# Spectrum's input and gate from one matmul of 170 columns a band, three tiles ahead, in one pair of PSUM banks

## The chip, the cores and the metric

One core of a Trainium2 chip runs the whole program. The metric is the device time of one execution in microseconds (us), the median of several runs; less is better. The engines are TensorE (PE, with its weight loads shown apart as PEld), VectorE (DVE), ScalarE (ACT), GpSimd (POOL) and SyncE (SP, which only issues DMAs). Each runs its own queue in order and waits for others by semaphores.

## What is computed

Two layers of the same block on x of shape (4, 32, 128, 128). Cut to what matters:

```
xn = group_norm(x)                        # 32 groups: each channel of each image by itself
xm = einsum('bchw,oc->bohw', xn, W_in)    # 32 channels -> 3 * 85
x_spatial, x_freq, x_gate = split(xm, 3)
out_spatial = depthwise_conv3x3(x_spatial, W_dw)
xf  = rfft2(x_freq in patches of 8 x 8) * fft_weight
out_freq = irfft2(xf)
x = x + einsum('bchw,oc->bohw', gelu(x_gate) * (out_spatial + out_freq), W_out)
```

The projection into x_spatial is merged with the depthwise convolution into one set of weights. The Fourier transform of a patch is a matmul with a basis over its pixels, and back another.

## The kernel before

**Tiles.** The image lies in SBUF with 128 partitions = 4 bands of 32 columns (q = 0 to 3) x 32 channels. A strip is 8 columns of each band over all 128 rows; there are 4 strips an image, 16 a layer, 32 in all. A strip has 8 tiles (TPS) of 16 rows x 8 columns = 128 pixels a band; 128 tiles (LT) a layer, 256 in all. A tile's matmuls take the pixels of one band as the stationary operand (128 x 128, with the high and low fp16 parts of the normalized input stacked on the partitions) and weights as the moving one, 85 columns (HID) a band. So a result of a tile is 128 pixels x 340 columns (GC, 4 bands x 85).

**What a tile goes through.** The names are the tiles of the trace.
- `ps_u` (L346): the input of the spectrum, four matmuls of 85 columns, one a band. ACT makes `uh` of it, its high fp16 part (L500), and DVE `ul`, the low part (L790, which reads `ps_u` and `uh`).
- `ps_z` (L406, 407, 409): three matmuls of 340 columns with the basis `bas`, on `uh`, `uh` and `ul`. DVE multiplies by the spectrum's weights into `y` (L796), ACT makes `yh` (L509) and POOL `yl` (L570).
- `ps_s` (L340): 7 matmuls of 85 columns a band for the convolution (`conv(i, q)`), then three of 340 with `inv` on `yh`, `yh` and `yl` (L414, 415, 417).
- `ps_g` (L346): the gate, four matmuls of 85 columns, from which ACT makes `g`, the gelu (L504). DVE multiplies `f` = `ps_s` x `g` (L764).
- `ps_ft` (L375): four transposes of `f`, which ACT copies to `ft` (L494). `ps_o` (L383): the output projection, once for two tiles, and DVE adds it to x (L774).

**The order.** Each engine runs the same loop over steps i = -3 to 259 (`steps()`, `live(i, offset)` says whether tile i + offset exists), each with its part written in a fixed order. PE in step i: conv of band 0 of tile i; transposes of tile i-2; in even steps `ps_o` of tiles i-4 and i-3; two of the four gate matmuls of tile i; conv of band 1; `ps_u` of tile i+3; the other two gate matmuls of tile i; conv of band 2; `ps_z` of tile i+2; conv of band 3; the three inverse matmuls into `ps_s`. ACT: `ft` of tile i-2, `uh` of i+3, `g` of i, `yh` of i+2. DVE: `f` of i-1, in odd steps the residual, `ul` of i+3, `y` of i+2. POOL: `yl` of i+2.

**Work beside the tiles.** The next strips' inputs are made in a strip's steps (`staged`): DVE normalizes (`norm`, L705, and an image's outer columns in L713) in step 0 of the strip, ahead of `ul`; ACT makes the high parts (`parts` L472) at the end of steps 1, 3 and 5, and DVE the low ones (L721) in steps 2, 4 and 6 ahead of `ul`, when ACT's copy is done. SP loads these into the `stack` tiles. In layer 0 DVE also makes statistics: two `bn_stats` (L669) in step 3 of each strip ahead of `ul`, for the strip that layer 0 has finished, and at the end of some early steps those of images 2 and 3 (L658), for which in step 1 it waits until the sums of image 1 have been sent: a DMA that POOL issues in step 0 behind `yl`. Layer 1's weights are merged on DVE and ACT (`scale`, `merge`, `hi_of_projection`, `hi_of_taps` and others, one each in steps 39 to 63) and laid out by ACT in 14 pieces (`placing`, L444, L451, L456) at the end of steps 7 and 0 of seven strips (steps 64 to 120).

**Buffers.** PSUM has eight banks, all in use: `ps_s` 2, `ps_u` 2, `ps_g`, `ps_z`, `ps_ft`, `ps_o` one each. `uh`, `ul`, `y`, `yh`, `yl`, `f`, `g` have two buffers each.

Of the kernel before, what the change touches and what calls it, by code (L numbers as in the profile page):

```python
# [7 lines left out]
F32 = mybir.dt.float32  # L8
F16 = mybir.dt.float16
I32 = mybir.dt.int32  # L10
ALU = mybir.AluOpType
# [28 lines left out]
HI, LO = 0, 1  # L40
LEAD = 3
DRAIN = 4
WARM = 40
KH = P * (P // 2 + 1)

# [30 lines left out]
def build(nc, x_in, edges_in, w_raw, w_fft, w_out, basis, inverse, eye32, fold, sums, y_out):  # L76
    ctx = ExitStack()
    with ctx:
        def sb(name, shape, dt=F32):
            return ctx.enter_context(nc.sbuf_tensor(name, shape, dt))  # L80

        def sem(name):
            return ctx.enter_context(nc.semaphore(name))
# [48 lines left out]

        uh = sb("uh", [128, 2, GC], F16)
        ul = sb("ul", [128, 2, GC], F16)
        g = sb("g", [128, 2, GC])
        y32 = sb("y32", [128, 2, GC])
        yh = sb("yh", [128, 2, GC], F16)
        yl = sb("yl", [128, 2, GC], F16)
# [3 lines left out]
        def bank(name):  # L142
            return ctx.enter_context(nc.psum_tensor(name, [128, 512], F32))
        ps_s = [bank("ps_s0"), bank("ps_s1")]
        ps_u = [bank("ps_u0"), bank("ps_u1")]
        ps_g, ps_z, ps_ft, ps_o = (bank(n) for n in ("ps_g", "ps_z", "ps_ft", "ps_o"))

        s_id = sem("s_id")
        s_basis = sem("s_basis")
# [46 lines left out]
        s_y = sem("s_y")  # L196
        s_yh = sem("s_yh")
        s_yl = sem("s_yl")
        s_gate = sem("s_gate")
        s_gelu = sem("s_gelu")  # L200
        s_s = sem("s_s")
        s_f = sem("s_f")
# [110 lines left out]
        def _(pe):  # L313
            mm = nc.tensor.matmul
            pe.wait_ge(s_id, 16)
            for l in range(LAYERS):
                pe.wait_ge(s_amax, l + 1)
                nc.tensor.transpose(ps_g[0:3, 128 * l:128 * l + 128], amax[:, l, :], id32[:, :]).then_inc(s_turned, 1)
                if l == 0:
                    pe.wait_ge(s_fold_in, 16)  # L320
                mm(ps_u[l][:, 0:HID], fold_sb[:, :], fft[l][:, :], start=True, stop=True).then_inc(s_fold, 1)
                pe.wait_ge(s_spread, l + 1)
                mm(ps_z[:, 4 * l:4 * l + 3], ones[:, :], spread[:, l, :], start=True, stop=True).then_inc(s_top, 1)
            pe.wait_ge(s_basis, 32)
# [6 lines left out]
            def pixels(kind, i, q, dy, rows=128):  # L331

                at = TW * (1 + TH * (i % TPS) + dy)
                return stack[(i // TPS) % 2][0:rows, kind, q, at:at + PIX]
# [5 lines left out]
                    mm(ps_s[i % 2][:, HID * q:HID * (q + 1)], pixels(kind, i, q, dy, rows), w[0:rows, m, :],  # L340
                       start=(q == 0 and m == 0), stop=False)

            def project(bank, which, i, bands):

                for q in bands:
                    t = mm(bank[:, HID * q:HID * (q + 1)], pixels(A, i, q, 0), pw[layer(i)][:, which, :],  # L346
                           start=(q == 0), stop=(q == Q - 1))
                return t

            def stacks_loaded(strip, kind):  # L350

# [10 lines left out]
            for i in steps():  # L362
# [21 lines left out]
                               start=True, stop=True)  # L384
                    o.then_inc(s_o, 1)
                if live(i, 0):
                    need(pe, s_gelu, i)
                    project(ps_g, 1, i, range(Q // 2))
                    conv(i, 1)
                if live(i, 3):  # L390
                    if (i + 3) % TPS == 0:
                        stacks_loaded((i + 3) // TPS, 0)
                    if (i + 3) % LT == 0:
                        pe.wait_ge(s_ready, PLACED * layer(i + 3) + PROJECTIONS)
                        pe.wait_ge(s_weff, LAYERS)
                    need(pe, s_uh, i + 2)
                    need(pe, s_ul, i + 2)
                    project(ps_u[(i + 3) % 2], 0, i + 3, range(Q)).then_inc(s_u, 1)
                if live(i, 0):
                    project(ps_g, 1, i, range(Q // 2, Q)).then_inc(s_gate, 1)  # L400
                    conv(i, 2)
                if live(i, 2):
                    k = i % 2
# [16 lines left out]
        def _(act):  # L420
# [66 lines left out]
            for i in steps():  # L487
                if i < 0:
                    for part in staged(i, {1: 1, 3: 3, 5: 5})[1]:
                        hi_part(1, ORDER[part // 2])  # L490
                if live(i, -2):
                    need(act, s_ftp, i - 1)
                    need(act, s_o, (i - 6) // 2 + 1)
                    nc.scalar.activation(ft[:, (i - 2) % 4, :, :].rearrange("p q n -> p (q n)"), ps_ft[0:HID, 0:Q * 128],  # L494
                                         ACT.Copy).then_inc(s_ft, 1)
                if live(i, 3):
                    k = (i + 3) % 2
                    need(act, s_u, i + 4)
                    need(act, s_z, i + 2)
                    nc.scalar.activation(uh[:, k, :], ps_u[k][:, 0:GC], ACT.Copy, scale=US).then_inc(s_uh, 1)  # L500
                if live(i, 0):
                    need(act, s_gate, i + 1)
                    need(act, s_f, i - 1)
                    nc.scalar.activation(g[:, i % 2, :], ps_g[:, 0:GC], ACT.Gelu,  # L504
                                         scale=gsc[layer(i)][:, 0:1]).then_inc(s_gelu, 1)
                if live(i, 2):
                    need(act, s_y, i + 3)
                    need(act, s_s, i + 1)
                    nc.scalar.activation(yh[:, i % 2, :], y32[:, i % 2, :], ACT.Copy).then_inc(s_yh, 1)  # L509
                strip, mine = staged(i, {1: 1, 3: 3, 5: 5})  # L510
                if i >= 0:
                    for part in mine:
                        hi_part(strip, ORDER[part // 2])

                if i == 40:
                    hi_of_projection(1)
                if i == 48:
                    hi_of_taps(1)
                if 64 <= i < LT - 8 and i % TPS in (0, TPS - 1):
                    placing(1, 2 * (i // TPS - 8) + (i % TPS == TPS - 1))  # L520
# [66 lines left out]
        def _(dve):  # L587
# [16 lines left out]
            def turned(l):  # L604

                dve.wait_ge(s_turned, l + 1)
                link(v.tensor_reduce(top[:, l:l + 1], ps_g[0:3, 128 * l:128 * l + 128], AX.X, ALU.max))
                dve.wait_ge(s_id, 16)
                v.tensor_scalar(spread[:, l, :], id32[0:3, 0:3], top[:, l:l + 1], None, ALU.mult).then_inc(s_spread, 1)

# [32 lines left out]

            def spectrum(l):
                dve.wait_ge(s_fold, l + 1)
                v.tensor_scalar(weff[l][:, :], ps_u[l][:, 0:HID], ip2[:, l, 1:2], 1.0 / (BS * BS * US),
                                ALU.mult, ALU.mult).then_inc(s_weff, 1)

            def image_stats(b, n):
# [108 lines left out]
            for i in steps():  # L758
                if live(i, -1):
                    k = (i - 1) % 2  # L760
                    need(dve, s_s, i)
                    need(dve, s_gelu, i)
                    need(dve, s_ftp, i - 2)
                    v.tensor_tensor(f[:, k, :], ps_s[k][:, 0:GC], g[:, k, :], ALU.mult).then_inc(s_f, 1)  # L764
                if live(i, -5) and i % 2 == 1:
                    tile = i - 5
                    l, b, k = place(tile // TPS)
# [17 lines left out]
                        lo_part(strip, ORDER[part // 2 - 1])  # L785
                if live(i, 3):
                    k = (i + 3) % 2
                    need(dve, s_uh, i + 4)
                    need(dve, s_z, i + 2)
                    v.scalar_tensor_tensor(ul[:, k, :], ps_u[k][:, 0:GC], US, uh[:, k, :],  # L790
                                           ALU.mult, ALU.subtract).then_inc(s_ul, 1)
                if live(i, 2):
                    k = i % 2
# [94 lines left out]
```

## Time and profile before

| | before |
|---|---|
| median of 3 runs | 861.08 us (860.65 to 861.73) |
| the profiled execution | 862.21 us, span 860.3 us, mean granted clock 0.989 |
| PE busy | 818.8 us, 95% of the span |
| PEld | 665.4 us, 77% |
| DVE | 616.5 us, 72% |
| ACT | 579.9 us, 67% |
| POOL | 264.7 us, 31% |
| the chain of work that ended last | PE 93%, DMA 3%, DVE 1%, ACT 1% |

The span runs from the first to the last instruction of the profiled execution. The chain goes back from the last instruction, at each step to what released it; its shares say which engine the end waited for. In a timeline row the first number is the start and the second the length; matmuls and the elementwise operations of ACT and DVE are pipelined, so that the next one starts before the last has ended: what one costs on a full queue is the distance from start to start, not its length.

### The profile page before, as it was taken

What the parts mean: (1) busy time and instruction counts of PE and PEld (TensorE: products, weight loads), DVE (VectorE), ACT (ScalarE), POOL (GpSimd) and SP (SyncE); (2) the same over time, 40 slices, a digit from 0 to 9 for tenths busy, and PEclk for the clock granted to TensorE, in tenths of its full rate; (3) what the DMA queues carried; (4) which work ended last, traced back from release to release, by engine and by line L of the source; (5) the groups of instructions that cost most, each with busy time, mean ns of one, the idle gap of its engine ahead of it and who ended that gap; (6) DMA issues with size and microseconds to landing.
All of it is one profiled execution on the core that took longest, in us unless ns stands there. A gap on an engine that the chain in (4) does not pass through costs nothing.

```text
span 860.3 us, 32550 instructions
## 1 busy us (share of the span) xinstructions
PE 818.8 (95%) x12850; PEld 665.4 (77%) x12850; DVE 616.5 (72%) x1198; ACT 579.9 (67%) x1154; POOL 264.7 (31%) x335
## 2 busy tenths in 40 slices
PE   1379999999999999999999999999999999999997
PEld 0258888888788888888888888878888888888886
DVE  6657877788787876778777776777766777667543
ACT  3246677666767777776776777677777767777664
POOL 1223224343334322243223422222222222232221
PEclk9969999999999999999999999999999999999999
DMA  7695446554445655544565555556565555655521
GB/s 268 139 252 153 116 114 144 126 131 114 114 116 115 145 123 126 118 117 105 116 139 134 126 132 144 135 129 154 136 153 148 132 129 133 160 133 147 134 77 51
DMA packets 65505, 115.66 MB, mean 134 GB/s; under 512 B 15874, under 2 KB 17066, under 8 KB 64970
## 3 DMA queue, kind: packets, MB, share of 16 engines
q1 hardware_dynamic: 62470, 109.71, 51.9%
q0 software_dynamic: 1904, 2.31, 1.1%
q8 instruction: 104, 1.70, 0.9%
q10 hardware_dynamic: 980, 1.55, 0.7%
q14 instruction: 47, 0.39, 0.1%
HBM read 11.01 MB, written 8.59 MB: 23 GB/s over the span
## 4 chain that ended last, share of the span: by engine, by line
PE 93%; DMA 3%; DVE 1%; ACT 1%; issue 1%; SPq 1%; POOL 0%; ACTq 0%; DVEq 0%; POOLq 0%
PE ps_s L340 34%; PE ps_ft L375 14%; PE ps_o L383 8%; PE ps_g L346 6%; PE ps_u L346 5%; PE ps_s L414 4%; PE ps_z L406 4%; PE ps_s L417 4%; PE ps_s L415 4%; PE ps_z L409 4%; PE ps_z L407 4%; DMA sums<-st 1%; DMA stack<-parts 1%; DMA id<-in_eye 1%; SPq L249 1%
## 5 line engine op out<-in xcount | busy, mean ns | idle before, releaser
L340 PE MATMUL ps_s<-cw,stack 128*128 128x85 f16 (+1 forms) x7168 | 458.8, 203 | 3.7 <-DVE f L764 3.7
L340 PEld LDWEIGHTS ps_s<-cw,stack 128*128 128x128 f16 (+1 forms) x7168 | 381.5, 99 | 53.2 <-DVE f L764 4.1
L570 POOL TENSOR_TENSOR yl<-y,yh 128x340 f16<-128x340 f32 x256 | 224.7, 878 | 561.2 <-ACT yh L509 561.2
L509 ACT ACTIVATE yh<-y 128x340 f16<-128x340 f32 x256 | 124.7, 487 | 206.0 <-DVE y L796 121.5
L790 DVE SCALAR_TENSOR_TENSOR ul<-ps_u,uh 128x340 f16<-128x340 f32 x256 | 130.0, 508 | 116.6 <-ACT uh L500 116.6
L721 DVE TENSOR_TENSOR parts<-xn,parts 128x1024 f16<-128x1024 f32 x96 | 117.5, 1226 | 90.0 <-ACT parts L472 90.0
L375 PE MATMUL ps_ft<-id,f 128*85 128x128 f32 x1024 | 163.1, 282 | 0.2 <-ACT ft L494 0.2
L494 ACT ACTIVATE ft<-ps_ft 85x512 f32<-85x512 f32 x256 | 149.7, 585 | 17.2 <-PE ps_ft L375 14.8
L764 DVE TENSOR_TENSOR f<-ps_s,g 128x340 f32<-128x340 f32 x256 | 129.1, 504 | 15.5 <-PE ps_s L417 5.4
L504 ACT ACTIVATE g<-ps_g,gsc 128x340 f32<-128x340 f32 x256 | 137.7, 538 | 0.8 <-PE ps_g L346 0.5
L500 ACT ACTIVATE uh<-ps_u 128x340 f16<-128x340 f32 x256 | 115.2, 450 | 22.8 <-PE ps_u L346 22.7
L796 DVE TENSOR_TENSOR y<-ps_z,weff 128x340 f32<-128x340 f32 x256 | 128.3, 501 | 1.3 <-PE ps_z L409 1.3
L346 PE MATMUL ps_g<-pw,stack 128*128 128x85 f16 x1024 | 126.0, 206 | 0.0
L346 PEld LDWEIGHTS ps_g<-pw,stack 128*128 128x128 f16 x1024 | 75.2, 99 | 53.4 <-issue 51.9
L375 PEld LDWEIGHTS ps_ft<-id,f 128*85 128x85 f32 x1024 | 115.2, 155 | 0.7 <-DVE f L764 0.7
L472 ACT ACTIVATE parts<-xn 128x1024 f16<-128x1024 f32 x96 | 99.9, 1043 | 15.1 <-issue 10.4
L346 PE MATMUL ps_u<-pw,stack 128*128 128x85 f16 x1024 | 81.9, 202 | 4.6 <-DMA stack<-parts 4.6
L383 PE MATMUL ps_o<-ft,wo 85*32 85x256 f32 x1024 | 81.8, 391 | 0.7 <-ACT ft L494 0.7
L406 PE MATMUL ps_z<-uh,bas 128*128 128x340 f16 x256 | 79.4, 310 | 2.3 <-DVE y L796 1.9
L414 PE MATMUL ps_s<-yh,inv 128*128 128x340 f16 x256 | 79.1, 309 | 0.0
L409 PE MATMUL ps_z<-ul,bas 128*128 128x340 f16 x256 | 79.1, 309 | 0.0
L407 PE MATMUL ps_z<-uh,bas 128*128 128x340 f16 x256 | 78.9, 308 | 0.0
(77 smaller groups left out, 632.8 us busy)
## 6 DMA issues: line engine op xcount, KB each, us to landing
stack<-parts SPq DMA_DIRECT2D x502, 130.0 KB, 2.6
stack<-parts SPq DMA_DIRECT2D x128, 65.0 KB, 2.0
out_y<-yo SPq DMA_DIRECT2D x16, 512.0 KB, 2.9
stack<-parts SPq DMA_DIRECT2D x124, 64.5 KB, 2.0
stack<-parts SPq DMA_DIRECT2D x124, 64.0 KB, 2.0
x<-in_x SPq DMA_DIRECT2D x3, 2048.0 KB, 10.1
x<-in_x SPq DMA_DIRECT2D x4, 512.0 KB, 6.9
gathered<-sums POOLq DMA_DIRECT2D x32, 24.0 KB, 2.7
```

What stands on the lines that cost most here:

```text
L340: mm(ps_s[i % 2][:, HID * q:HID * (q + 1)], pixels(kind, i, q, dy, rows), w[0:rows, m, :], start=(q == 0 and m == 0), stop=False)
L346: t = mm(bank[:, HID * q:HID * (q + 1)], pixels(A, i, q, 0), pw[layer(i)][:, which, :], start=(q == 0), stop=(q == Q - 1))
L375: t = nc.tensor.transpose(ps_ft[0:HID, q * 128:(q + 1) * 128], f[:, k, HID * q:HID * (q + 1)], id32[:, :])
L383: o = mm(ps_o[C * q:C * q + C, 0:256], wo[layer(i - 4)][:, :], ft[:, k:k + 2, q, :], start=True, stop=True)
L494: nc.scalar.activation(ft[:, (i - 2) % 4, :, :].rearrange("p q n -> p (q n)"), ps_ft[0:HID, 0:Q * 128], ACT.Copy).then_inc(s_ft, 1)
L504: nc.scalar.activation(g[:, i % 2, :], ps_g[:, 0:GC], ACT.Gelu, scale=gsc[layer(i)][:, 0:1]).then_inc(s_gelu, 1)
L509: nc.scalar.activation(yh[:, i % 2, :], y32[:, i % 2, :], ACT.Copy).then_inc(s_yh, 1)
L570: nc.gpsimd.tensor_tensor(yl[:, k, :], y32[:, k, :], yh[:, k, :], ALU.subtract).then_inc(s_yl, 1)
L721: v.tensor_tensor(part[:, LO], xn[:, :, 1 + dx:1 + dx + TW], part[:, HI], ALU.subtract).then_inc(s_xl, 1)
L764: v.tensor_tensor(f[:, k, :], ps_s[k][:, 0:GC], g[:, k, :], ALU.mult).then_inc(s_f, 1)
L790: v.scalar_tensor_tensor(ul[:, k, :], ps_u[k][:, 0:GC], US, uh[:, k, :], ALU.mult, ALU.subtract).then_inc(s_ul, 1)
L796: v.tensor_tensor(y32[:, k, :].rearrange("p (q o) -> p q o", q=Q), ps_z[:, 0:GC].rearrange("p (q o) -> p q o", q=Q), weff[layer(i + 2)][:, ...
```

## The change

One matmul of 170 columns a band makes the spectrum's input and the gate together (`pw` holds both sets of weights side by side), four a tile instead of eight of 85. They write `ps_ug`, two banks of PSUM in one tensor: band q at column 256 q, its first 85 columns the spectrum's input (`ps_u`, now a view of it) and the next 85 the gate (`ps_g`). There is one such pair of banks, no second buffer, and no bank `ps_g` of its own; seven banks are used.

The projection of tile i+3 stays where `ps_u`'s was in step i, behind conv of band 1; both gate pieces of tile i go away. PE waits ahead of it for `ul` and `g` of tile i+2. On ACT `g` of tile i+3 follows `uh` of tile i+3 at once, under the same wait for `s_u`. On DVE `ul` waits for `g` of its tile instead of `uh`, so that ACT and DVE don't read the pair of banks together. `g` has five buffers (AHEAD = LEAD + 2), since `f` uses it four steps later; `f` no longer waits for `s_gelu`. Operations that read `ps_ug` go over four runs of 85 elements. Two small matmuls and a transpose at the program's start write other banks.

PE, a step without `ps_o`, before, from the start of conv of band 0:

```order
L340 MATMUL ps_s<-cw,stack 128x85 [waits s_f]
L340 MATMUL ps_s<-cw,stack 128x85 x6
L375 MATMUL ps_ft<-id,f 85x128 [waits s_ft,s_f]
L375 MATMUL ps_ft<-id,f 85x128 x3
L346 MATMUL ps_g<-pw,stack 128x85 [waits s_gelu]
L346 MATMUL ps_g<-pw,stack 128x85
L340 MATMUL ps_s<-cw,stack 128x85 x7
L346 MATMUL ps_u<-pw,stack 128x85 [waits s_ul,s_uh]
L346 MATMUL ps_u<-pw,stack 128x85 x3
L346 MATMUL ps_g<-pw,stack 128x85 x2
L340 MATMUL ps_s<-cw,stack 128x85 x7
```

and the same place now:

```order
L344 MATMUL ps_s<-cw,stack 128x85 [waits s_f]
L344 MATMUL ps_s<-cw,stack 128x85 x6
L380 MATMUL ps_ft<-id,f 85x128 [waits s_ft,s_f]
L380 MATMUL ps_ft<-id,f 85x128 x3
L344 MATMUL ps_s<-cw,stack 128x85 x7
L351 MATMUL ps_ug<-pw,stack 128x170 [waits s_gelu,s_ul]
L351 MATMUL ps_ug<-pw,stack 128x170 x3
L344 MATMUL ps_s<-cw,stack 128x85 x7
```

Eight matmuls in three places have become four in one, and its waits are for the tile before, in the same banks.

DVE, one step's `ul` and `y` and what stands ahead and behind, before:

```order
L721 TENSOR_TENSOR parts<-xn,parts 128x1024 [waits s_xh,s_xn]
L790 SCALAR_TENSOR_TENSOR ul<-ps_u,uh 128x340 [waits s_z,s_uh]
L796 TENSOR_TENSOR y<-ps_z,weff 128x340 [waits s_yl,s_z]
L764 TENSOR_TENSOR f<-ps_s,g 128x340 [waits s_ftp,s_gelu,s_s]
L774 SCALAR_TENSOR_TENSOR x<-ps_o,osc,x 128x32x8 [waits s_o]
```

and now:

```order
L722 TENSOR_TENSOR parts<-xn,parts 128x1024 [waits s_xh,s_xn]
L790 SCALAR_TENSOR_TENSOR ul<-ps_ug,uh 128x340 [waits s_z,s_gelu]
L797 TENSOR_TENSOR y<-ps_z,weff 128x340 [waits s_yl,s_z]
L764 TENSOR_TENSOR f<-ps_s,g 128x340 [waits s_ftp,s_s]
L774 SCALAR_TENSOR_TENSOR x<-ps_o,osc,x 128x32x8 [waits s_o]
```

The order is the same; the wait for `g` has moved from `f` to `ul`. ACT's order (`ft`, `uh`, `g`, `yh`, `parts`) is unchanged too.

```diff
-        ps_u = [bank("ps_u0"), bank("ps_u1")]
-        ps_g, ps_z, ps_ft, ps_o = (bank(n) for n in ("ps_g", "ps_z", "ps_ft", "ps_o"))
+        ps_z, ps_ft, ps_o = (bank(n) for n in ("ps_z", "ps_ft", "ps_o"))
+        ps_ug = ctx.enter_context(nc.psum_tensor("ps_ug", [128, 1024], F32))
+        bands = ps_ug[:, :].rearrange("p (q n) -> p q n", q=Q)
+        ps_u, ps_g = bands[:, :, 0:HID], bands[:, :, HID:2 * HID]
...
-            def project(bank, which, i, bands):
-                for q in bands:
-                    t = mm(bank[:, HID * q:HID * (q + 1)], pixels(A, i, q, 0), pw[layer(i)][:, which, :],
-                           start=(q == 0), stop=(q == Q - 1))
-                return t
+            def project(i):
+                for q in range(Q):
+                    at = 256 * q
+                    t = mm(ps_ug[:, at:at + 2 * HID], pixels(A, i, q, 0), pw[layer(i)][:, :, :],
+                           start=(q % 2 == 0), stop=(q % 2 == 1))
+                t.then_inc(s_u, 1)
...
                 if live(i, 0):
-                    need(pe, s_gelu, i)
-                    project(ps_g, 1, i, range(Q // 2))
                     conv(i, 1)
                 if live(i, 3):
...
-                    need(pe, s_uh, i + 2)
-                    need(pe, s_ul, i + 2)
-                    project(ps_u[(i + 3) % 2], 0, i + 3, range(Q)).then_inc(s_u, 1)
+                    need(pe, s_ul, i + 3)
+                    need(pe, s_gelu, i + 3)
+                    project(i + 3)
                 if live(i, 0):
-                    project(ps_g, 1, i, range(Q // 2, Q)).then_inc(s_gate, 1)
                     conv(i, 2)
...
                     need(act, s_u, i + 4)
                     need(act, s_z, i + 2)
-                    nc.scalar.activation(uh[:, k, :], ps_u[k][:, 0:GC], ACT.Copy, scale=US).then_inc(s_uh, 1)
-                if live(i, 0):
-                    need(act, s_gate, i + 1)
-                    need(act, s_f, i - 1)
-                    nc.scalar.activation(g[:, i % 2, :], ps_g[:, 0:GC], ACT.Gelu,
-                                         scale=gsc[layer(i)][:, 0:1]).then_inc(s_gelu, 1)
+                    nc.scalar.activation(uh[:, k, :].rearrange("p (q o) -> p q o", q=Q), ps_u, ACT.Copy,
+                                         scale=US).then_inc(s_uh, 1)
+                    need(act, s_f, i + 4 - AHEAD)
+                    nc.scalar.activation(g[:, (i + 3) % AHEAD, :].rearrange("p (q o) -> p q o", q=Q), ps_g,
+                                         ACT.Gelu, scale=gsc[layer(i + 3)][:, 0:1]).then_inc(s_gelu, 1)
...
                     need(dve, s_s, i)
-                    need(dve, s_gelu, i)
                     need(dve, s_ftp, i - 2)
-                    v.tensor_tensor(f[:, k, :], ps_s[k][:, 0:GC], g[:, k, :], ALU.mult).then_inc(s_f, 1)
+                    v.tensor_tensor(f[:, k, :], ps_s[k][:, 0:GC], g[:, (i - 1) % AHEAD, :], ALU.mult).then_inc(s_f, 1)
...
-                    need(dve, s_uh, i + 4)
+                    need(dve, s_gelu, i + 4)
                     need(dve, s_z, i + 2)
-                    v.scalar_tensor_tensor(ul[:, k, :], ps_u[k][:, 0:GC], US, uh[:, k, :],
+                    v.scalar_tensor_tensor(ul[:, k, :].rearrange("p (q o) -> p q o", q=Q), ps_u, US,
+                                           uh[:, k, :].rearrange("p (q o) -> p q o", q=Q),
                                            ALU.mult, ALU.subtract).then_inc(s_ul, 1)
```

## Rows read from the trace of the kernel before

**Rows 1.** The page, part 1: busy us, share of the span, instructions.
```profile
PE 818.8 (95%) x12850; PEld 665.4 (77%) x12850; DVE 616.5 (72%) x1198; ACT 579.9 (67%) x1154; POOL 264.7 (31%) x335
```

**Rows 2.** The list of waits: who for whom, total us, times, longest.
```profile
PE ps_s L340 <- DVE f L764: 3.7, 1, 3.7
```

**Rows 3.** The timeline of PE, steps 119 to 121: start, length, operation.
```profile
401.48 0.64 PE L375 MATMUL ps_ft<-id,f 128*85 128x128 f32 x4
...
402.32 0.32 PE L346 MATMUL ps_u<-pw,stack 128*128 128x85 f16 x4
402.47 0.24 PE L346 MATMUL ps_g<-pw,stack 128*128 128x85 f16 x2
402.55 0.45 PE L340 MATMUL ps_s<-cw,stack 128*128 128x85 f16 x7
402.84 0.31 PE L406 MATMUL ps_z<-uh,bas 128*128 128x340 f16 x1
...
403.27 0.45 PE L340 MATMUL ps_s<-cw,stack 128*128 128x85 f16 x7
...
404.27 0.64 PE L375 MATMUL ps_ft<-id,f 128*85 128x128 f32 x4
...
407.74 0.64 PE L375 MATMUL ps_ft<-id,f 128*85 128x128 f32 x4
```

**Rows 4.** The timeline of ACT, steps 119 to 126.
```profile
402.67 0.46 ACT L500 ACTIVATE uh<-ps_u 128x340 f16<-128x340 f32 x1
...
414.14 0.49 ACT L509 ACTIVATE yh<-y 128x340 f16<-128x340 f32 x1 [0.86 <-DVE y L796]
...
421.13 0.58 ACT L494 ACTIVATE ft<-ps_ft 85x512 f32<-85x512 f32 x1
421.61 0.44 ACT L500 ACTIVATE uh<-ps_u 128x340 f16<-128x340 f32 x1
421.95 0.54 ACT L504 ACTIVATE g<-ps_g,gsc 128x340 f32<-128x340 f32 x1
423.05 0.49 ACT L509 ACTIVATE yh<-y 128x340 f16<-128x340 f32 x1 [0.56 <-DVE y L796]
423.44 1.04 ACT L472 ACTIVATE parts<-xn 128x1024 f16<-128x1024 f32 x1
424.39 0.57 ACT L494 ACTIVATE ft<-ps_ft 85x512 f32<-85x512 f32 x1
```

**Rows 5.** The timeline of DVE, steps 122 to 126.
```profile
413.61 0.50 DVE L796 TENSOR_TENSOR y<-ps_z,weff 128x340 f32<-128x340 f32 x1
...
416.16 0.49 DVE L790 SCALAR_TENSOR_TENSOR ul<-ps_u,uh 128x340 f16<-128x340 f32 x1
...
422.08 0.51 DVE L790 SCALAR_TENSOR_TENSOR ul<-ps_u,uh 128x340 f16<-128x340 f32 x1 [0.57 <-ACT uh L500]
422.51 0.50 DVE L796 TENSOR_TENSOR y<-ps_z,weff 128x340 f32<-128x340 f32 x1
...
424.58 1.23 DVE L721 TENSOR_TENSOR parts<-xn,parts 128x1024 f16<-128x1024 f32 x1 [1.10 <-ACT parts L472]
425.73 0.50 DVE L790 SCALAR_TENSOR_TENSOR ul<-ps_u,uh 128x340 f16<-128x340 f32 x1
```

**Rows 6.** The timeline of ACT around a piece of layer 1's weights.
```profile
379.21 0.49 ACT L509 ACTIVATE yh<-y 128x340 f16<-128x340 f32 x1 [0.69 <-PE ps_s L417]
...
380.16 0.59 ACT L494 ACTIVATE ft<-ps_ft 85x512 f32<-85x512 f32 x1
```

**Rows 7.** The timeline of DVE from step 47 to 48.
```profile
203.36 0.50 DVE L796 TENSOR_TENSOR y<-ps_z,weff 128x340 f32<-128x340 f32 x1
...
206.86 0.50 DVE L790 SCALAR_TENSOR_TENSOR ul<-ps_u,uh 128x340 f16<-128x340 f32 x1
```

**Rows 8.** The timelines of DVE and PE at the first steps.
```profile
59.49 0.69 DVE L658 BATCH_NORM_STATS2 st<-x 128x6 f32<-128x512 f32 x1 [5.45 <-DMA sums<-st]
...
60.66 0.68 PE L340 MATMUL ps_s<-cw,stack 128*128 128x85 f16 x7 [3.73 <-DVE f L764]
```

More of the change, by code:

```diff
@@ L42 @@
 DRAIN = 4
+AHEAD = LEAD + 2
 WARM = 40
@@ L134, in build @@
         ul = sb("ul", [128, 2, GC], F16)
-        g = sb("g", [128, 2, GC])
+        g = sb("g", [128, AHEAD, GC])
         y32 = sb("y32", [128, 2, GC])
@@ L198, in build @@
         s_yl = sem("s_yl")
-        s_gate = sem("s_gate")
         s_gelu = sem("s_gelu")
@@ L317, in _ @@
                 pe.wait_ge(s_amax, l + 1)
-                nc.tensor.transpose(ps_g[0:3, 128 * l:128 * l + 128], amax[:, l, :], id32[:, :]).then_inc(s_turned, 1)
+                nc.tensor.transpose(ps_o[0:3, 128 * l:128 * l + 128], amax[:, l, :], id32[:, :]).then_inc(s_turned, 1)
                 if l == 0:
                     pe.wait_ge(s_fold_in, 16)
-                mm(ps_u[l][:, 0:HID], fold_sb[:, :], fft[l][:, :], start=True, stop=True).then_inc(s_fold, 1)
+                mm(ps_ug[:, HID * l:HID * l + HID], fold_sb[:, :], fft[l][:, :], start=True, stop=True).then_inc(s_fold, 1)
                 pe.wait_ge(s_spread, l + 1)
@@ L606, in turned @@
                 dve.wait_ge(s_turned, l + 1)
-                link(v.tensor_reduce(top[:, l:l + 1], ps_g[0:3, 128 * l:128 * l + 128], AX.X, ALU.max))
+                link(v.tensor_reduce(top[:, l:l + 1], ps_o[0:3, 128 * l:128 * l + 128], AX.X, ALU.max))
                 dve.wait_ge(s_id, 16)
@@ L645, in spectrum @@
                 dve.wait_ge(s_fold, l + 1)
-                v.tensor_scalar(weff[l][:, :], ps_u[l][:, 0:HID], ip2[:, l, 1:2], 1.0 / (BS * BS * US),
+                v.tensor_scalar(weff[l][:, :], ps_ug[:, HID * l:HID * l + HID], ip2[:, l, 1:2], 1.0 / (BS * BS * US),
                                 ALU.mult, ALU.mult).then_inc(s_weff, 1)
```

## The prediction

> **What bounds the kernel now.** I read the page first: TensorE (PE) is busy 95% of the span, ScalarE (ACT) and VectorE (DVE) 67% and 72% [rows 1]. Then the list of waits: once its loads are in, PE waits only for `f`, once, 3.7 us [rows 2]; all else that waits is ACT, DVE or POOL. So from about 61 us on PE sets the time. The PE timeline gives its beat: the transposes start at 401.48, 404.27 and 407.74, so a step without the `ps_o` matmuls takes 2.79 us and one with them 3.47 us, 6.26 for two tiles, 25.04 for the eight tiles of a strip and 801 for 32 strips [rows 3]. The work around it (loads, first steps, last transposes and store) makes 860.3. The median of the runs, 861.1, lies 0.8 above this span and the profiled run's own time, 862.2, 1.9 above; I add what the sum gives for the span to the median.
>
> **The change on PE.** A step had eight matmuls of 85 columns. Start to start the four into `ps_u` take 0.15 us, the two into `ps_g` behind them 0.08, the two ahead 0.09, in all 0.32, 40 ns each; seven conv matmuls take 0.29, 41 ns each. The three of 340 columns from 402.84 on take 0.43, 0.145 each [rows 3]. A 170-column one has no row. It lies between half of a 340 one (72 ns) and two 85 ones (80 ns); a straight line through both sizes gives 40 + (145 - 40) x 85/255 = 75 ns, nearly what I take, 74, because the 340 spacing alternates 0.14 and 0.15. Four are 0.296: 0.024 us a step less, between 0 and 0.033. PE's strip becomes 25.04 - 0.19 = 24.85, its two steps 2.77 and 3.44.
>
> A rule of the Trainium skill speaks here too. The rows show 85 columns at 40 to 41 ns and 340 at 145 ns [rows 3]. "TensorE: Matmul & The Clock Gate", section "Back-to-back issue gap", gives the gap of a matmul alone as columns/2.4 + 2.5 ns. An estimate by it is 38, 73 and 144 ns for 85, 170 and 340 columns, so four for eight would give back only 0.01 us a step (2.5 us in all) against 0.024 by the rows; the 85-column row contradicts it by 2 to 3 ns and the 340 row agrees. The same section gives some 81 ns for 128 columns in a stream of weight loads and matmuls, which these rows don't show.
>
> **The change elsewhere, which decides.** Three waits change. PE may write the one pair of banks for tile i+3 only when both `ul` and `g` of tile i+2 are made (before: two `ps_u` banks, a tile more of slack). `g` of tile i+3 is now made directly behind `uh` of it. And DVE's `ul` waits for `g`, no longer for `uh`. Behind `ul` on DVE stands `y`; behind `y` waits ACT's `yh`, and behind `yh` on ACT stand the `parts` copy, `ft` and the next `uh`. So there is now a ring ft, uh, g (ACT), ul, y (DVE), yh (ACT), ft, through which each tile must go, and in which ACT can't work on anything else while DVE makes `ul` and `y`. Before, `g` ran on ACT (421.95) while DVE made `ul` (422.08) [rows 4, 5]: `g` was no part of the ring.
>
> Its price, start to start, from rows where the next instruction had nothing to wait for: ft to uh 0.48, uh to g 0.34, g 0.54 long [rows 4], hand-over to DVE 0.03 (uh ends 422.05, ul starts 422.08), ul to y 0.43 [rows 5], y 0.50 long, hand-over back 0.03 (413.61 + 0.50, yh at 414.14), yh to the next on ACT 0.39 [rows 4]. Sum 2.74 us. A `parts` copy adds 0.95 three times in a strip [rows 4]. The `lo` part on DVE that follows it hides: copy 1.04 + 0.03, then 1.14 to `ul` [rows 4, 5], is 2.21, against 0.95 + 0.48 + 0.34 + 0.57 = 2.34 on ACT. So the ring takes 8 x 2.74 + 2.85 = **24.77 us a strip**, against 24.85 for PE: a tie. Without `g` in it it had been some 0.44 a step shorter (`ul` started 0.03 after `uh`'s end), 21.3 a strip.
>
> Does PE wait in a plain strip? `uh` starts 0.35 after PE's first `ps_u` matmul (402.32, 402.67 [rows 3, 4]), now 0.15 later for four of 74 ns: P + 0.50. `ul` starts at P + 1.41 and ends at P + 1.92, and PE can go on about 0.1 later (an estimate: the hand-over of 0.03 and a weight load), at P + 2.0, where its own next projection stands at P + 2.77. The slack is 0.77. From step 0 to 6 of a strip the ring takes 6 x 2.74 + 2.85 = 19.29 and PE 3 x 2.77 + 3 x 3.44 = 18.63; the lag of 0.66 just fits. So in layer 1, where ACT and DVE have only this, PE still bounds: -0.19 a strip. That ring and PE are within 0.1 us a strip is the weak place of this forecast.
>
> In layer 0 other work stands in the ring:
> - Once a strip (steps 11 to 131) DVE makes two `bn_stats` ahead of `ul`: y 413.61 to ul 416.16 is 2.55 by DVE alone [rows 5], against 0.53 + 0.39 + 0.48 + 0.34 + 0.57 = 2.31 by ACT. +0.24: strip 25.0, longer than PE's 24.85, about what it was before (-0.05).
> - In steps 64 to 120 ACT writes layer 1's weights, two pieces a strip, 14 in all. The one between 379.21 and 380.16 costs 380.16 - 379.21 - 0.39 = 0.56 [rows 6]; the fourteen read so cost 0.31 to 0.56 and come to 6.4, 0.91 a strip. Before, they lay in ACT's idle time (0.69 ahead of each `yh` [rows 6]). Strip 25.9, +0.87, for 7 strips **+6.1**.
> - Single pieces. The longest is in step 48, where statistics, the merging of the taps and a norm with its edge stand on DVE between `y` and `ul`: 206.86 - 203.36 = 3.50, over 2.31 by 1.2 [rows 7]. Read in the same way, DVE's step 40 costs 1.0, and ACT's `vh` and `wh` of layer 1 0.7 and 0.3. +3.2 in all.
>
> The sum: start of the program +0.7 (0 to 2: `yl` of tile 2 comes later by the `g` in the ring, behind it on POOL stands the DMA of the sums, whose landing DVE and then PE await until 59.49 and 60.66 [rows 8]); plain strips 16 x -0.19 = -3.0, and -0.5 for the last three tiles' gates, which are made earlier; six and a half strips with statistics -0.3; weights +6.1; single pieces +3.2; going from PE's beat to the ring's and back once gains 2.77 - 2.0 = -0.7. Together **+5.5**: span 865.8, median 866.6.
>
> **Nothing for:** the dropped wait of `f` for `g` (`g` is now three tiles early), the five `g` buffers, and the startup matmuls in other banks (before 42 us PE waits for loads anyway). The reads of `ps_ug` in four runs of 85 have no row; the `parts` copies, whose input goes in runs of 8 elements, cost 0.95 for 1024 elements, as contiguous `ft` costs 0.48 for 512 [rows 4], so I take nothing, and 10 ns an operation as an upper bound, 30 ns a step.
>
> **Rivals.**
> (1) Ends faster: PE stays the bound throughout, because ACT's pieces are absorbed. It decides if the ring is at least 0.15 us a step shorter than 2.74 (the 25.9 of the weights' strips less 24.85, by 8). For it: PE's beat is rock steady now, and an error of 20 ns a step moves 2.5 us of layer 0. Against: `yh` can't start before `y`, and the queue orders are unchanged. It gives -0.024 x 253 = -6 and the last gates -0.5: 854.6.
> (2) Near no change: the ring is 20 to 40 ns a step shorter, or half of the single pieces hide: 866.6 - 3 - 2.5 = 861 to 862.
> (3) Clearly slower: the ring costs 30 ns a step more (reads in four runs, or waits between ACT and DVE that cost more when both are always late). A strip's ring is then 25.0, 0.16 over PE's, so it bounds layer 1 too: 16 x 0.16 = 2.6 there and 16 x 0.24 = 3.8 in layer 0 on top of the forecast: 873.
> (4) The change doesn't do what it says: a 170-column matmul costs 80 ns as two of 85. Then layer 1 is as before: +3.5, 870.
>
> **How the numbers follow.** The forecast (863 to 870, with (4) inside it) has 0.48, (3) 0.12, (2) 0.18, (1) and what lies between 854 and 859 0.22. The time is 866.6; the range 855 to 875 leaves out the outer parts of (1) and (3). What a measurement can tell from no change is 0.2%, 1.7 us. Slower 0.60, same 0.17, faster 0.23.
>
> **What would show it.** Right: matmuls into `ps_ug` come every 74 ns; in layer 0 PE waits at the projection for `ul`, most between 258 and 432 us, where a strip takes 25.9; in layer 1 a strip takes 24.85 with hardly a wait; ACT's `yh` waits for `y` at every step. Wrong: no waits in layer 0 (rival 1), or waits in layer 1 too (rival 3); strips of 25.04 there with none (4).

## The result, and the profile after

| | before | changed |
|---|---|---|
| median | 861.0 us (860.65 to 861.73) | 871.6 us (870.68 to 871.91) |
| profiled execution, its span | 862.2, 860.3 us | 871.8, 870.0 us |

The changed kernel takes 1.012 of the time before (95% interval 1.0103 to 1.0138): slower by 10.6 us. The forecast was slower, by 5.5 (866.6). The spans of the two profiled executions differ by less than the medians, 9.7 us, because the one before ran 1.2 above its median and the changed one 0.2.

The page of the changed kernel, parts 1 and 4, against [rows 1]:

```profile
PE 819.4 (94%) x11826; PEld 661.1 (76%) x11826; DVE 608.8 (70%) x1198; ACT 555.9 (64%) x1154; POOL 263.4 (30%) x335
PE 67%; ACT 13%; DVE 9%; issue 7%; DMA 2%; SPq 1%; ACTq 0%; DVEq 0%; POOL 0%; POOLq 0%
```

By busy time nothing has become the bound: PE is still at 94%, ACT and DVE are even a little less busy. But the chain of work that ended last was 93% PE before and is 67% PE now, with 13% of ACT and 9% of DVE in it. The list of waits, whose counterpart is [rows 2] (who for whom, us in total, times, longest):

```profile
ACT yh L510 <- DVE y L797: 265.1, 253, 5.6
DVE ul L790 <- ACT g L505: 143.8, 131, 7.0
PE ps_ug L351 <- DVE ul L790: 6.4, 13, 1.5
```

`yh` waits for `y` in 253 of its 256 times (135 before), and `ul` now waits for `g`. PE's own waits look small, because a matmul that waits for a few tenths of a us behind a pipelined predecessor is partly counted as busy (an example is below). The start of the first projection matmul of every eighth tile shows them better. From those starts in the two traces:

| stretch (tiles) | before, us | changed, us | difference | forecast |
|---|---|---|---|---|
| to tile 8 | 70.58 | 71.47 | +0.9 | +0.7 |
| 8 to 64: statistics, single pieces | 175.26 | 178.71 | +3.5 | +2.9 |
| 64 to 128: weights of layer 1 | 200.29 | 207.88 | +7.6 | +6.1 |
| 128 to 248: layer 1 | 375.60 | 373.84 | -1.8 | -2.9 |
| rest, to the end | 38.6 | 38.1 | -0.5 | -0.5, -0.1 for the strip in it, and -0.7 for the change of bound |
| span | 860.3 | 870.0 | +9.7 | +5.5 |

The places are those of the forecast. Every one of the sizes came out on the slow side of it, by 0.2, 0.6, 1.5, 1.1 and 0.8 us (the 0.7 for the change of bound has no place of its own and stands in the last row).

The ring in the timeline of ACT, then of DVE, in layer 1 (steps 176 and 177; before: [rows 4, 5]):

```profile
617.91 0.45 ACT L502 ACTIVATE uh<-ps_ug 128x340 f16<-128x340 f32 x1
618.26 0.54 ACT L505 ACTIVATE g<-ps_ug,gsc 128x340 f32<-128x340 f32 x1
619.79 0.49 ACT L510 ACTIVATE yh<-y 128x340 f16<-128x340 f32 x1 [1.00 <-DVE y L797]
620.18 0.57 ACT L496 ACTIVATE ft<-ps_ft 85x512 f32<-85x512 f32 x1
```
```profile
618.83 0.51 DVE L790 SCALAR_TENSOR_TENSOR ul<-ps_ug,uh 128x340 f16<-128x340 f32 x1
619.26 0.50 DVE L797 TENSOR_TENSOR y<-ps_z,weff 128x340 f32<-128x340 f32 x1
```

`g` ends at 618.80, `ul` starts 0.03 later, `y` ends at 619.76 and `yh` starts 0.03 later: ACT stands idle for 1.00 us between `g` and `yh`, and so in every plain step. `uh` took 0.45 and `g` 0.54 as before, though they read four runs of 85 across two banks.

Two of PE's stretches, one in layer 1 (step 171) and one in the strips with weights (step 75):

```profile
601.51 0.46 PE L351 MATMUL ps_ug<-pw,stack 128*128 128x170 f16 x4
601.80 0.45 PE L344 MATMUL ps_s<-cw,stack 128*128 128x85 f16 x7
```
```profile
294.55 0.45 PE L344 MATMUL ps_s<-cw,stack 128*128 128x85 f16 x7
295.30 0.47 PE L351 MATMUL ps_ug<-pw,stack 128*128 128x170 f16 x4 [0.30 <-DVE ul L790]
```

Four matmuls of 170 columns take 0.29 us (601.51 to 601.80). In the second, the seven conv matmuls are through 0.29 after 294.55, and the projection starts 0.75 after it: some 0.46 us lost, of which the row shows 0.30 as idle.

### The profile page after: what moved, and what is told of

The parts are those of the page before. It is cut to its first block, busy times and chain, and to the rows that moved or that the text cites. A ratio compares the mean times of both kernels' runs of the same rounds, so it can differ in the third digit from the quotient of the medians.

```text
span 870.0 us, 30247 instructions
## 1 busy us (share of the span) xinstructions
PE 819.4 (94%) x11826; PEld 661.1 (76%) x11826; DVE 608.8 (70%) x1198; ACT 555.9 (64%) x1154; POOL 263.4 (30%) x335
## 4 chain that ended last, share of the span: by engine, by line
PE 67%; ACT 13%; DVE 9%; issue 7%; DMA 2%; SPq 1%; ACTq 0%; DVEq 0%; POOL 0%; POOLq 0%
PE ps_s L344 25%; PE ps_ft L380 10%; PE ps_ug L351 7%; PE ps_o L388 6%; DVE y L797 4%; ACT ft L496 3%; ACT parts L474 3%; PE ps_s L416 3%; PE ps_z L408 3%; ACT g L505 3%; PE ps_s L417 3%; PE ps_s L419 3%; PE ps_z L409 3%; PE ps_z L411 3%; ACT uh L502 2%
## 5 line engine op out<-in xcount | busy, mean ns | idle before, releaser
L344 PEld LDWEIGHTS ps_s<-cw,stack 128*128 128x128 f16 (+1 forms) x7168 | 392.3, 99 | 106.9 <-issue 51.9
L790 DVE SCALAR_TENSOR_TENSOR ul<-ps_ug,uh 128x340 f16<-128x340 f32 x256 | 130.5, 510 | 144.4 <-ACT g L505 143.8
L496 ACT ACTIVATE ft<-ps_ft 85x512 f32<-85x512 f32 x256 | 147.3, 575 | 4.5 <-PE ps_ft L380 4.3
L505 ACT ACTIVATE g<-ps_ug,gsc 128x340 f32<-128x340 f32 x256 | 137.0, 535 | 0.3
L351 PE MATMUL ps_ug<-pw,stack 128*128 128x170 f16 x1024 | 118.8, 238 | 15.6 <-DVE ul L790 6.4
L502 ACT ACTIVATE uh<-ps_ug 128x340 f16<-128x340 f32 x256 | 112.6, 440 | 7.7 <-PE ps_ug L351 7.3
L351 PEld LDWEIGHTS ps_ug<-pw,stack 128*128 128x128 f16 x1024 | 73.0, 98 | 21.7 <-DVE ul L790 8.4
L419 PE MATMUL ps_s<-yl,inv 128*128 128x340 f16 x256 | 78.6, 307 | 0.0
```

The lines of the kernel that those rows point to most:

```text
L351: t = mm(ps_ug[:, at:at + 2 * HID], pixels(A, i, q, 0), pw[layer(i)][:, :, :], start=(q % 2 == 0), stop=(q % 2 == 1))
L502: nc.scalar.activation(uh[:, k, :].rearrange("p (q o) -> p q o", q=Q), ps_u, ACT.Copy, scale=US).then_inc(s_uh, 1)
L505: nc.scalar.activation(g[:, (i + 3) % AHEAD, :].rearrange("p (q o) -> p q o", q=Q), ps_g, ACT.Gelu, scale=gsc[layer(i + 3)][:, 0:1]).then_ ...
L790: v.scalar_tensor_tensor(ul[:, k, :].rearrange("p (q o) -> p q o", q=Q), ps_u, US, uh[:, k, :].rearrange("p (q o) -> p q o", q=Q), ALU.mul ...
```

## Experiments

The theory under test, the **ring**: the time is lost because `g` now stands between `uh` and `ul`, so that ft, uh, g, ul, y, yh make one chain over two engines. First rival, the **bank**: it is lost because PE has only one pair of banks to write and must wait for both of its readers. Second rival, the **price**: the wide matmul, or the reads in four runs, cost more than their predecessors.

### y ahead of ul

```diff
 DVE, a step
-    ul (tile i+3), waits s_gelu
-    y (tile i+2)
+    y (tile i+2)
+    ul (tile i+3), waits s_gelu
```

> The changed kernel with DVE making y of tile i+2 ahead of ul of tile i+3, nothing else moved. Ring theory (the time was lost because g stands in the chain ft, uh, g, ul, y, yh): y and yh no longer stand behind g, the chain is cut, PE bounds in both layers with strips of 24.91 us, 31 x 0.13 less than before and the last gates 0.4 less, start up to 0.9 more: 856 to 858. Bank theory (the time was lost because PE waits for the only pair of banks): ul comes 0.25 later, so PE waits more often: 872 to 880. Price theory (170 columns or reads in four runs cost more): 871 to 872, unchanged.

Measured: 858.6 us, 0.9976 of before (0.9965 to 0.9988), 0.6 above the upper end of what the ring theory gave. With the two operations exchanged the changed kernel is 13 us faster than it was, and faster than before. Strips take 24.89 to 24.91 in both layers (one of 25.30, that of step 48). Its waits:

```profile
DVE y L790 <- PE ps_z L411: 147.6, 147, 2.1
ACT yh L510 <- PE ps_s L419: 141.3, 229, 1.9
ACT yh L510 <- DVE y L790: 23.1, 26, 5.0
```

`y` and `yh` wait for PE again, not for each other. PE still has one pair of banks. In a plain strip `ul`, which frees it, starts 1.64 us behind the projection in every step; in the changed kernel it is 1.41 in step 0 of a strip, where the ring has not yet fallen behind, and 2.02 in step 6. So the pair is free neither always earlier nor always later than in the changed kernel, and it does not hold PE, whose strips are at 24.89 to 24.91. What settles the bank theory is the wait alone, below. The start was late, tile 8's projection at 72.91 in place of 71.47.

### g behind ul

```diff
 DVE
-    need(dve, s_gelu, i + 4)        # ahead of ul
+    need(dve, s_uh, i + 4)
 ACT
+    need(act, s_ul, i + 4)          # ahead of g
```

> The changed kernel with ul waiting for uh, and g waiting for ul (one more wait on ACT ahead of g), so that ACT and DVE still never read the pair of banks together. Ring theory: the chain is ft, uh, ul, then g and y side by side, 2.33 us a step in place of 2.74, 21.5 a strip, PE bounds everywhere: 856 to 859. Bank theory: the banks come free at 2.1 us after PE's projection in place of 2.0, so PE waits a little more: 872 to 876. Price theory: unchanged, 871 to 872.

Measured: 862.1 us, 1.0014 (1.0004 to 1.0023). 9.5 us come back, and 3 more were expected: in layer 1 strips take 24.91, in layer 0 24.95 to 25.65, and tile 8 starts at 72.35. Here ACT must wait for `ul` (188 us in all, 256 times) ahead of `g`, and `yh` stands behind it. The ring is shorter, not gone. It points the same way as the first: the less of the chain stands behind `g`, the less is lost. The 3 us lie in layer 0 (tiles 8 to 128 take 376.2 us, in y first 373.8) and were not taken apart.

### The wait alone, in the kernel before

```diff
 need(dve, s_uh, i + 4)
+need(dve, s_gelu, i + 1)
 need(dve, s_z, i + 2)
```

> The kernel before with one wait added: DVE's ul of tile i+3 also waits for g of tile i (which ACT makes directly behind uh of tile i+3). 85-column matmuls, two ps_u banks and ps_g stay. Ring theory: the same chain as in the changed kernel, the same losses in layer 0 (3 us in strips 1 to 7, 7.6 in the strips with layer 1's weights), layer 1 as before with 25.04: 869 to 873. Bank theory and price theory: no change from before, 861.

Measured: 880.7 us, 1.023 (1.0213 to 1.0247), 8 above the upper end of what the ring theory gave, and far from the 861 of the rivals. With 85-column matmuls, two `ps_u` banks and `ps_g`, the one wait costs 20 us. There are two `ps_u` banks here and no 170-column matmul, so neither the bank nor the price is needed for such a loss. The excess over the changed kernel starts in the trace of ACT:

```profile
622.23 0.54 ACT L504 ACTIVATE g<-ps_g,gsc 128x340 f32<-128x340 f32 x1
623.82 0.49 ACT L509 ACTIVATE yh<-y 128x340 f16<-128x340 f32 x1 [1.05 <-DVE y L797]
```

From `g` to `yh` are 1.59 us, in the changed kernel 1.53. The 0.06 lie between `g`'s end and `ul`: 0.089 against 0.032 us. `ul` has three waits here and two there. Eight times 0.06 a strip makes the ring 25.2 us, over PE's 25.04, so it bounds in layer 1 too (strips of 25.16 to 25.24 at the end). Tiles 128 to 248 take 3.0 us more than in the kernel before; tiles 8 to 64 and 64 to 128 take 2.0 and 3.4 more than in the changed kernel.

### Eight matmuls of 85 in the changed kernel

```diff
-t = mm(ps_ug[:, at:at + 2 * HID], pixels(A, i, q, 0), pw[layer(i)][:, :, :], ...)
+for which in range(2):
+    t = mm(ps_ug[:, at + HID * which:at + HID * which + HID], pixels(A, i, q, 0), pw[layer(i)][:, which, :], ...)
```

> The changed kernel with eight matmuls of 85 columns into the same places of the pair of banks in place of four of 170, in the same place of PE's order. Ring theory: layer 0 hardly moves, since ACT and DVE bound it; layer 1's strips go from 24.91 to 25.04 or a little more, 16 x 0.15 = +2.4: 873 to 875. Price theory, if 170 columns were the cause: faster than the changed kernel, 865 or less.

Measured: 874.3 us, 1.0158 (1.0141 to 1.0175). Tiles 8 to 128 take 386.9 us, in the changed kernel 386.6: in layer 0 the matmuls don't matter. In layer 1 strips take 25.07 in place of 24.91. The price theory falls as to the matmul, which is a gain; as to the reads in four runs, which this kernel keeps, it falls with the lengths of `uh`, `g` and `ul` and with the wait alone, which has no such reads.

### Without layer 1's weights

> The changed kernel without the 14 pieces in which ACT lays out layer 1's weights in steps 64 to 120; layer 1 computes with layer 0's weights. Ring theory: strips 8 to 15 fall from 25.99 to 25.0 us on average, -7.6: 864. If the waits in those strips came from something else (the single pair of banks, contention): 870 or more.

```diff
-if 64 <= i < LT - 8 and i % TPS in (0, TPS - 1):
-    placing(1, 2 * (i // TPS - 8) + (i % TPS == TPS - 1))
```

Measured: 864.7 us, 1.0054 (1.0039 to 1.0069). Tiles 64 to 128 take 201.33 in place of 207.88. The pieces of weights cost the changed kernel 6.9 us of time, 6.5 of it in this stretch, where they cost the kernel before nothing: its strips take 25.04 us with them and without. But 201.33 is still 1.0 more than in the kernel before.

### The statistics behind y

> The changed kernel with the two bn_stats of step 3 of a strip moved on DVE from ahead of ul to behind y, where nothing of the ring stands behind them but f and the lo part, which must wait for ACT's copy anyway. Ring theory: 0.24 us less in each of 15 strips that the ring bounds, -3 to -4: 868. If DVE's work as a sum were the limit, its place would not matter: 871.6.

```diff
 DVE, step 3 of a strip
     residual
-    bn_stats x2
     ul
     y
+    bn_stats x2
```

Measured: 868.2 us, 1.0098 (1.0081 to 1.0115), 3.4 less than the changed kernel, as expected. Tiles 8 to 128 take 383.8 in place of 386.6. The same 1.3 us of work on DVE costs 0.19 us a strip more ahead of `ul` than behind `y` (2.8 over 15 strips):

```profile
297.17 0.51 DVE L787 SCALAR_TENSOR_TENSOR ul<-ps_ug,uh 128x340 f16<-128x340 f32 x1 [0.94 <-ACT g L505]
297.60 0.50 DVE L794 TENSOR_TENSOR y<-ps_z,weff 128x340 f32<-128x340 f32 x1
298.01 1.28 DVE L670 BATCH_NORM_STATS2 st<-x 128x6 f32<-128x512 f32 x2
```

DVE waits 0.94 us for `g` again where before the two `bn_stats` had stood.

### Neither

The two edits above together. As in the kernel without the pieces, layer 1's own weights are never laid out, and layer 1 runs on layer 0's.

> Without the 14 pieces of weights (layer 1 computes with layer 0's) and with the bn_stats behind y. Ring theory: both savings add, -11: 860 to 861, still above y first (858.6), since the single pieces of steps 39 to 63 stay in the ring. If the two hide each other: 864.

Measured: 861.9 us, 1.002 (1.0009 to 1.003), 9.7 less than the changed kernel; 10.2 would be the sum of the two, and 11 had been expected. Tiles 8 to 64 still take 177.3, 2.0 over the kernel before; 25.78 and 26.64 are the strips of steps 37 to 53, where most of the single pieces are.

### y ahead of ul, and eight matmuls of 85

> y ahead of ul, and eight matmuls of 85 columns in place of four of 170. With the ring cut PE bounds everywhere, so this tells what the wide matmul is worth: strips of 25.07 as in the kernel with eight matmuls (in layer 1) in place of 24.91: 31 x 0.16 = +5 over y first, 863 to 864. If the wide matmul were worth nothing: 858.6.

Measured: 864.0 us, 1.0047 (1.0031 to 1.0064). Strips take 25.06 or 25.07 where y first has 24.89 to 24.91. So with the ring cut, the wide matmul is worth 5.4 us against eight of 85 in its place. Against the kernel before, where the eight stood in three places and a strip took 25.04, it is 0.13 to 0.15 a strip.

### Pieces that start at partition 0

In the rows of the weights' strips of the changed kernel one distance was out of line:

```profile
289.15 0.34 ACT L446 ACTIVATE pw<-wh 32x170 f16<-32x170 f16 x1
289.52 0.59 ACT L496 ACTIVATE ft<-ps_ft 85x512 f32<-85x512 f32 x1
290.01 0.44 ACT L502 ACTIVATE uh<-ps_ug 128x340 f16<-128x340 f32 x1
290.48 0.54 ACT L505 ACTIVATE g<-ps_ug,gsc 128x340 f32<-128x340 f32 x1
```

From `uh` to `g` are 0.47 us, where it is 0.34 elsewhere. In both traces that is so behind the ten pieces that begin at partition 32, 64 or 96, and not behind the four that begin at 0. The next kernel is the one without pieces with 14 copies put in their places:

```diff
+nc.scalar.activation(spare[0:32, 3 x 85], (vh, vl)[n % 2][0:32, n % 3::3, :], ACT.Copy).then_inc(s_ready, 1)
```

> The changed kernel where the 14 pieces of weights are replaced by 14 copies of 32 x 255 elements in the same places of ACT's order, all of which read and write from partition 0 (into a spare tile; layer 1 computes with layer 0's weights). In the traces so far a piece that starts at partition 32, 64 or 96 costs 0.42 to 0.56 us itself and makes the distance from uh to g behind it 0.46 in place of 0.34, one that starts at partition 0 costs 0.31 and nothing behind it. If the partition is the cause: 14 x 0.31 = 4.3 over the kernel without pieces (864.7): 869. If any such small copy does it: 14 x 0.56 + 14 x 0.13 = 9.7 at most, 872 or more.

Measured: 868.6 us, 1.01 (1.0082 to 1.0119); tiles 64 to 128 take 204.5, 3.2 more than without pieces and 3.4 less than with the real ones. The same place in its trace:

```profile
391.42 0.40 ACT L475 ACTIVATE spare<-vh 32x255 f16<-32x255 f16 x1
391.72 0.57 ACT L505 ACTIVATE ft<-ps_ft 85x512 f32<-85x512 f32 x1
392.20 0.43 ACT L511 ACTIVATE uh<-ps_ug 128x340 f16<-128x340 f32 x1
392.53 0.52 ACT L514 ACTIVATE g<-ps_ug,gsc 128x340 f32<-128x340 f32 x1
```

0.30 for the piece and 0.33 from `uh` to `g`, behind all fourteen. So where the piece starts is what counts. (The 0.31 that the expectation gives for a piece at partition 0 is that of 32 x 255 elements, the size of these copies; the two smaller sizes cost 0.23 and 0.16.) Whether it is the partition that it reads from or the one that it writes to is not told apart: in the real pieces the two are the same.

### The sums of image 1 sent early

```diff
-GATHER[1] = 0
+GATHER[1] = -LEAD
```

This starts the exchange of image 1's statistics in step -3. First in y first:

> y ahead of ul, and the statistics of image 1 sent, gathered and used three steps earlier, so that POOL issues the DMA of the sums ahead of yl of tile 0 and not behind yl of tile 2. In y first, DVE waits 4.8 us for its landing and PE 3.4 us for DVE. If that DMA alone holds PE: 3 us less than y first, 855 to 856. If the loads of the second strip's stack, which land until 64 us, take its place: 857 to 858.6.

Measured: 854.2 us, 0.9932 (0.9919 to 0.9944), better than expected; tile 8's projection stands at 66.43 in place of 72.91, of which the runs' medians keep 4.4 us (the profiled execution of y first ran 1.7 above its median). PE's 3.4 us of waiting for `f` at the start are gone, and so is DVE's wait ahead of its first statistics in the loop:

```profile
56.61 0.68 DVE L659 BATCH_NORM_STATS2 st<-x 128x6 f32<-128x512 f32 x1
```

Then in the kernel before:

> The kernel before with the statistics of image 1 sent, gathered and used three steps earlier, nothing else. This tells how much of the 6.4 us by which y first with the early send beats the kernel before is due to the early send alone. In the kernel before, PE waits 3.7 us for what stands behind that DMA; y first gained 4.4 by it. If the two gains simply add: 861 - 4 = 857, and y first with the wide matmul keeps 3 us over it. If the early send brings all of it: 854.

Measured: 856.0 us, 0.995 (0.9933 to 0.9966), between the two values. Most of the gain of the fastest kernel is this line's. The wide matmul with y first keeps 1.9 us over it, where the strips promise 4 (31 x 0.13): its start is 1.9 later (66.43 against 64.52). In the first steps each projection waits for the readers of the one pair of banks: PE stands idle for 1.5, 1.0 and 1.1 us ahead of those of tiles 1, 2 and 3. Here the pair of banks does cost something.

Why does a wait of 3.7 us [rows 2] cost tile 8 of the kernel before 6.1 us (70.58 against 64.52)? The granted clock of TensorE tells. In the kernel before it is 1.2 GHz from 59.4 us, when PE has been waiting since 56.9, until 66.2, and 2.4 GHz from there on. Two matmuls of 340 columns each, first under the low clock, then under the high one:

```profile
63.63 0.49 PE L406 MATMUL ps_z<-uh,bas 128*128 128x340 f16 x1
63.91 0.49 PE L407 MATMUL ps_z<-uh,bas 128*128 128x340 f16 x1
...
68.31 0.31 PE L406 MATMUL ps_z<-uh,bas 128*128 128x340 f16 x1
68.46 0.30 PE L407 MATMUL ps_z<-uh,bas 128*128 128x340 f16 x1
```

One takes 0.28 us in place of 0.15. From 61 to 65 us PE gets through 42 matmuls at a granted clock of 0.50; in the kernel before with the early send it gets through 76, at 1.00. All eleven traces in which PE waits here, for 2.7 to 4.4 us, show such a fall, for 3.4 or 6.8 us; the two with the early send have none from 55 us to the last 2 us of the program. So the early send took away the wait and the slow stretch behind it, and my expectation for it had counted the wait alone.

## Why the prediction was right, point by point

The direction and the cause were right: `g` in the ring of hand-overs, no loss in layer 1, the loss where other work stands in the ring. The size was about half: +5.5 for +10.6, with every stretch of the table on the low side. The range held it by its width.

- **What bounds**: right. The beat of 25.04 a strip held over the whole trace of the kernel before.
- **The ring**: right, and its price in a plain strip too. The sum was 2.74 us a step; in layer 1 of the changed kernel the links measure 0.48, 0.33, 1.53 (from `g` to `yh`) and 0.39, together 2.73. `ul` starts 1.41 after the projection in step 0 of a strip, as worked out, and 2.02 in step 6: the lag was to be 0.66 and is 0.61. The slack was enough, by some 0.18 us (`ul` ends 0.24 ahead of the next projection; where PE does wait, the projection starts 0.06 behind `ul`'s end, for which I had estimated 0.1), and layer 1 stayed with PE. Y first and the wait alone show it from both sides.
- **The statistics**: right, 3.4 us come back when they are moved (in the trace 0.19 us a strip, for 0.24 in the sum).
- **The weights' pieces**: right in mechanism, and near in size partly by luck. In the stretch with them the term was +6.1 and the trace has +7.6. The kernel without pieces splits this. The pieces themselves cost 6.5 there, and I had 6.4. Two errors offset in it: I priced a piece from `yh` to `ft` and stopped there, as if it cost nothing behind the next operation, but ten of the fourteen delay `g` by another 0.13 (290.01 to 290.48 above), 1.3 us in all; and I took all of a piece as lost, where some of it is absorbed (the fourteen at partition 0, 0.305 each, 4.3 us together, cost 3.2). The delay of `g` stood in the trace of the kernel before as well, in which ACT's idle time covered it. What I had too low is the strip without pieces, 25.0 by my sum, a little under the 25.04 of before: in the kernel without pieces it is 25.17, for the eight 1.0 more than before. With the statistics moved too it is 24.99 (199.94 for the eight, PE alone being at 24.89). What holds the strips up beyond pieces and statistics was not taken apart.
- **Layer 1's gain**: mis-sized, -1.8 us for -2.9. The matmuls that I priced did what I took them for. From start to start over 72 steps of layer 1 (tiles 160 to 232) the eight of 85 columns took 0.320 us a step before and the four of 170 take 0.294, 0.026 less. What the sum had at nothing is their neighbours: the 28 conv matmuls of a step take 1.147 in place of 1.138. Seven of them take 0.284 behind two gate matmuls, where two of the four groups stood. Now one of these groups stands behind the wide matmuls (0.286) and the other behind the transposes (0.286) or, in every second step, behind `ps_o` (0.296). The strip lost 0.13, 0.017 a step in place of 0.024.
- The rule of the Trainium skill ("TensorE: Matmul & The Clock Gate", "Back-to-back issue gap") bears on the same term. Columns/2.4 + 2.5 ns gives 38 and 73; the four `ps_u` matmuls have 38 and `ps_ug` 74. But eight of 85 in a row take 0.318 in the kernel with eight matmuls, 40 each, so that four for eight save 0.024 and not the 0.01 that was estimated by the rule. That the step as a whole gained 0.017, between the two, is the doing of conv.
- **Single pieces and the early strips**: +3.5 for +2.9. The kernel with neither pieces nor statistics in the ring still has 2.0 of it. Not taken apart further. The 0.7 us that the change of bound was to give back are not seen as an item of their own; the stretch from tile 8 on holds both.
- **The start**: right in mechanism: POOL issues the sums' DMA behind `yl` of tile 2 at 54.70 in place of 52.66, and DVE goes on at 61.19 in place of 59.49 [rows 8], 1.7 later. The size, +0.9 for +0.7, is luck. Tile 8 is later by less than 1.7, and what differs is the clock: TensorE was granted 1.2 GHz for 3.4 us behind the wait (63.4 to 66.8), and for 6.8 in the trace before. The landing of the DMA differs by run too: with the same ring, the kernel with eight matmuls went on at 59.76 and had tile 8 at 70.28. What I didn't see there was that this DMA's place was worth 4.4 us to the kernel before.
- **Rivals**: (1) and (2) fell, since `yh` waits for `y` at 253 steps and the ring is as long as summed; PE throughout came only with the order on DVE changed, which is no part of (1). (4) fell with the 0.29 of the four matmuls. Of (3) the mechanism, hand-overs that cost more, was seen, but in another kernel: the wait alone.

## What to carry to other kernels

When a change puts two outputs in one bank and the kernel keeps their readers on two engines apart, one reader follows the other, and that order becomes part of every chain that goes through either. Before making it, write down the ring of hand-overs over all in-order queues, sum it from start-to-start distances, and compare it with the beat of the bounding engine; here busy shares of 64 to 70% hid a ring at 99% of PE's beat. The cure was no buffer and no faster operation but to take out of the ring, on the queue that waits, the one operation that doesn't need what it waits for. And a wait of the bounding engine is not priced by its length alone: look at the granted clock behind it.

## What the runs showed of the hardware

- An ACT operation that starts on another partition quarter (0, 32, 64 or 96) than its neighbours costs more than its length. From `yh` to `ft`, less the 0.39 without a piece, 32 x 85, 32 x 170 and 32 x 255 elements cost 0.42, 0.49 and 0.56 us when they start at partition 32, 64 or 96, and 0.16, 0.23 and 0.31 when they start at 0; and `g` comes 0.13 later behind the former, though `ft` and `uh` stand between. The Trainium skill has a rule for VectorE, "VectorE: DVE Perf Modes", section "Two Vector instructions with no wait between them": an instruction of which an input or the output starts in another quarter than the last one in that memory did is held until all earlier ones have finished. Applied to ACT it fits all the rows: the piece is held, `ft` behind it (output in SBUF), not `uh` (input in PSUM), and `g` again, whose scale `gsc` is the next input from SBUF. The page states it for VectorE alone; the pieces at partition 0, with neither delay, agree.
- A hand-over from `g`'s end to `ul`'s start took 0.032 us with two waits on `ul` (the changed kernel) and 0.089 with three (the wait alone). That the number of waits is the cause was not tested apart.
- Reading PSUM in four runs of 85 elements over two banks costs ACT and DVE nothing: `uh` 440, `g` 535, `ul` 510 ns on average, before 450, 538 and 508.
- A matmul's spacing in this stream of weight loads at 2.4 GHz: 38 to 41 ns for 85 columns, 73 to 76 for 170, 143 to 147 for 340. The first group behind `ps_o`, fp32 matmuls, takes 10 ns longer than the same behind the fp32 transposes (seven conv matmuls 0.296 against 0.286 us).
- A wait of PE of 2.7 to 4.4 us early in the program was followed or accompanied by 3.4 or 6.8 us at 1.2 GHz in all eleven traces that have it. Wait and slow stretch together cost the kernel before 6.1 us at tile 8, where the wait itself was 3.7. Between executions the mean granted clock goes with the time: of the kernel before, those at 0.994 took 858.7 to 859.5 us, those at 0.987 861.5 to 862.3.
